# One operation over two neighbouring PSUM banks, for ScalarE's exponentials and VectorE's maxima in two attention stages

## The chip, the cores and the metric

The kernel runs on one core of a Trainium2 chip. The metric is the device time of one execution in microseconds (us). The five engines run their own queues and meet at semaphores: PE (TensorE) writes matmul results to PSUM, ACT (ScalarE) and DVE (VectorE) read PSUM and write SBUF, POOL (GpSimd) and SP (SyncE) have nothing to do in the two stages of this case.

PSUM holds eight banks here, each of 512 fp32 values per partition. A bank is filled by PE, signalled full, emptied by ACT or DVE, and signalled done.

## The reference, cut to what matters

Four layers run one after the other on x of 32 x 256 rows of 128 values (64 tiles of 128 rows): a delta-rule attention, a mixture of experts, a sliding-window attention and a full attention with a second mixture. Only the two softmax attentions are touched:

```python
# sliding window, W = 64 keys per query, 16 heads of 8
scores = jnp.einsum('blhd,blwhd->blwh', q, k_win) * dh ** (-0.5)
attn = jax.nn.softmax(scores, axis=2)
out = jnp.einsum('blwh,blwhd->blhd', attn, v_win).reshape(b, l, d)
...
# full attention inside each sequence of 256, 16 heads of 8
scores = jnp.einsum('bqhd,bkhd->bhqk', q, k) / np.sqrt(DK)
attn = jax.nn.softmax(scores, axis=-1)
o = jnp.einsum('bhqk,bkhd->bqhd', attn, v).reshape(B, S, D)
```

## The kernel before, in words

`attention_stage` is called twice, as the window stage (names ending in `_win`) and as the full stage (`_full`). Each walks 64 tiles of 128 rows; two tiles make a turn (one sequence of 256), two turns a loop body. The scores are computed twice per tile. `scores` puts queries on partitions, so that DVE can take each query's largest score (`maxima`); the maxima are turned (`turn_tops`) and added to the queries through a spare row (`tops`). `turned_scores` then computes keys on partitions with that maximum already taken off, ACT takes the exponential (`exponentials`), and `weigh` multiplies by the values. The row sums come out of a column of ones in `va`; `turn_back` and `normalize_out` divide by them.

The 16 heads lie in 4 groups (GROUPS) of 4 slots. A fill of scores takes four banks at once, one for each group. In the window stage a tile has one such fill of each kind (SF = TF = 4), in the full stage two (SF = TF = 8).

What sets the order is written out by hand: each engine has its own program, and four rings of banks with a full and a done counter each. The `scores` ring uses banks 2, 3, 0, 1, the `turned_scores` ring banks 2, 3, 4, 5; so banks 2 and 3 serve both. Bank 6 goes to ACT (`am`), bank 7 to DVE (`dv`). `scores` waits until the first two banks of the last turned fill are done (`st.filled - 2`), and `turned_scores` until the first two of the last scores fill are (`sc.filled - 2`). `fill_together` waits for all four of its own ring's last fill, `weigh` and `turn_tops` wait for all banks of a tile. Every one of these thresholds is an even number of banks.

In a tile of the full stage PE's order is: second scores (L2597), `turn_back` (L2655), either two query projections (L2556) or the turning of h (L2549), second turned scores (L2626), `turn_tops` (L2662), `turn_on` (L2668), the next first scores (L2597), `weigh` (L2646), first turned scores (L2626), `project_out` (L2674, L2676), then values (L2570) or keys and queries (L2563, L2556). The maxima are L2834 in the full stage and L2831 in the window stage, the exponentials L2765. Below, a tile that turns h is called an h tile, one that projects queries a q tile; they alternate, so that there are 32 of each.

Of the kernel before, what the change touches and what calls it, by code (L numbers as in the profile page):

```python
# [15 lines left out]
F32 = mybir.dt.float32  # L16
BF16 = mybir.dt.bfloat16
ACT = mybir.ActivationFunctionType
AX = mybir.AxisListType.X

P = 128
# [62 lines left out]
def start_signals(engine, *signals):  # L84

    for s in signals:
        engine.sem_inc(s.sem, s.per)
# [2267 lines left out]
SEQ = TPB * P  # L2355
GROUPS = 4
SLOTS = H1 // GROUPS
SETS = 2
GROUP = P // GROUPS
TOP_ROW = 2 * DH  # L2360
# [95 lines left out]
def attention_stage(nc, c, x_all, mid, w, tiles, tag, window, take=None):  # L2456
# [15 lines left out]
    KEYS = 2 * WIN - 1 if window else P  # L2472
    SCALE = DH ** -0.5
    SF, TF = (4, 4) if window else (8, 8)
    VB = 4 if window else 2
    with ExitStack() as ctx:
        def sb(name, shape, dt=F32):
            return ctx.enter_context(nc.sbuf_tensor(f"{name}_{tag}", shape, dt))
# [20 lines left out]
        mxp = sb("mxp", [P, SLOTS, P])  # L2499
        pr = sb("pr", [P, 2, TF, 512])  # L2500
# [7 lines left out]
        with ExitStack() as early:  # L2508
# [1 line left out]
                                zeros=(wq, wk, qb, va, mxp, hT, mr[:, :, tiles:], x_all[:, tiles + 1:, :],  # L2510
                                       x_all[:, 0, :], *(() if mid is None else (mean[:, :, 0], mid[:, 0, :]))),
                                ones=(oT, ones))
        bank = [ctx.enter_context(nc.psum_tensor(f"bank_{tag}_{i}", [P, 512], F32)) for i in range(8)]

        sc = Ring(ctx, nc, f"scores_{tag}", [bank[i] for i in (2, 3, 0, 1)], SF * U, ahead=SF + 4)
        st = Ring(ctx, nc, f"turned_{tag}", bank[2:6], TF * U, ahead=4)
# [220 lines left out]
        @block.scalar  # L2737
        def _(act):
            start_signals(act, st.done, am.done)

            def turned_h(b):
                bk = am.empty(act, b)
                if window:
                    nc.scalar.activation(hT[:, LEAD:], bk[:, 0:SEQ], ACT.Copy).then_inc(am.done.sem, 1)
                else:
                    nc.scalar.activation(hT[:, :], bk[:, 0:SEQ], ACT.Identity, scale=w["ln"][:, 0:1],
                                         bias=w["ln"][:, 1:2]).then_inc(am.done.sem, 1)

            def queries(b, p, half):
                bk = am.empty(act, b)  # L2750
                if window:
                    nc.scalar.activation(q[:, p, 2 * half:2 * half + 2, :],
                                         bk[:, :].rearrange("p (s n) -> p s n", s=2), ACT.Copy).then_inc(am.done.sem, 1)
                else:
                    for i in range(2):
                        slot = 2 * half + i
                        ins = nc.scalar.activation(q[:, p, slot, :], bk[:, i * SEQ:(i + 1) * SEQ], ACT.Identity,
                                                   bias=qb[:, slot:slot + 1])
                    ins.then_inc(am.done.sem, 1)

            def exponentials(b, u, n):
                for _ in range(n):
                    i = st.emptied % TF
                    bk = st.empty(act, b)
                    nc.scalar.activation(pr[0:KEYS, u % 2, i, :], bk[0:KEYS, :], ACT.Exp, scale=SCALE  # L2765
                                         ).then_inc(st.done.sem, 1)

            def copy(b, dst):
                bk = am.empty(act, b)
                nc.scalar.activation(dst, bk[:, 0:dst.shape[-1]], ACT.Copy).then_inc(am.done.sem, 1)  # L2770

            turned_h(0)
            queries(0, 0, 0)
            queries(0, 0, 1)
            turned_h(0)
            queries(0, 1, 0)
            exponentials(0, 0, 4)
            with act.Fori(0, bodies) as b:
                for u in range(U):
                    p, t = u // TPB % 2, u % TPB  # L2780
                    if t == 0:
                        queries(b, 1 - p, 1)
                    else:
                        turned_h(b)
                    if not window:
                        exponentials(b, u, 4)
                    copy(b, onT[:, :])
                    copy(b, oT[:, :])
                    exponentials(b, u + 1, 4)
                    if t == 1:  # L2790
                        queries(b, p, 0)
            copy(bodies - 1, onT[:, :])

        @block.vector
        def _(dve):
# [28 lines left out]
                    ins.then_inc(dv.done.sem, 1)  # L2824

            def maxima(b, first):
                for g in range(GROUPS):
                    bk = sc.empty(dve, b)
                    at = g * GROUP + TOP_ROW
                    if window:  # L2830
                        dve.tensor_reduce(mxp[:, :, at], bk[:, 0:SLOTS * KEYS].rearrange("p (s k) -> p s k", s=SLOTS),  # L2831
                                          AX, ALU.max).then_inc(sc.done.sem, 1)
                    else:
                        dve.tensor_reduce(mxp[:, 2 * first:2 * first + 2, at],  # L2834
                                          bk[:, :].rearrange("p (s k) -> p s k", s=2), AX, ALU.max
                                          ).then_inc(sc.done.sem, 1)

            def tops(b, u):

# [33 lines left out]
            for i in range(SF // 4):  # L2873
                maxima(0, i)
            tops(0, 0)
            keys(0, 1)
            maxima(0, 0)
            with dve.Fori(0, bodies) as b:
                for u in range(U):
                    turn, t = divmod(u, TPB)  # L2880
                    p = turn % 2
                    if not window:
                        maxima(b, 1)
                    normalize_out(b, u + 1)
                    tops(b, u + 1)
                    maxima(b, 0)
                    add_out(b, u, u)
                    if t == 0:
                        values(b, 1 - p)
                        norm_h(b, turn + 2, am_use(u - 1, "hT") if u else 4)  # L2890
                    else:
                        keys(b, p)
# [6 lines left out]
def window_stage(nc, c, x_all, a, tiles, take):  # L2899
    with ExitStack() as ctx:  # L2900
# [20 lines left out]
        with ExitStack() as s:  # L2921
# [15 lines left out]
            def _(pe):  # L2937
# [3 lines left out]
        w = {"wq": wt[:, 0, :], "wk": wt[:, 1, :], "wv": wt[:, 2, :], "wo": wo[:, :], "last_k": last_k,  # L2941
             "last_v": last_v}
        attention_stage(nc, c, x_all, None, w, tiles, "win", True, take)


def full_stage(nc, c, x_all, mid_all, a, tiles):
    with ExitStack() as ctx:
# [9 lines left out]
        with ExitStack() as s:  # L2957
# [4 lines left out]
            def _(dve):  # L2962
# [13 lines left out]
        w = {"wq": wqkv[:, 0:P], "wk": wqkv[:, P:2 * P], "wv": wqkv[:, 2 * P:], "wo": wo[:, :], "ob": ob[:, :],  # L2976
             "vb": vb[:, :], "qkb": qkb, "ln": ln}
        attention_stage(nc, c, x_all, mid_all, w, tiles, "full", False)


# [155 lines left out]
```

## Time and profile before

| what | before |
|---|---|
| median of 3 runs | 7614.07 us |
| all three | 7606.62, 7614.07, 7653.81 us |
| profiled execution | 7602.55 us, its span 7600.8 us |
| busy in the span | PE 84%, DVE 51%, ACT 41% |
| maxima, full stage | 524 of 685 ns |
| exponentials, full stage | 516 of 602 ns |
| maxima, window stage | 264 of 681 ns |
| exponentials, window stage | 260 of 602 ns |

A time is the whole execution; the span is the profiled part of it, and 1.75 us lie around it. Of the span, the window stage's tiles take from about 5420 to 6150 us and the full stage's from about 6205 to 6994 us; the rest belongs to the other stages.

### The profile page before, as it was taken

The numbers are of one execution on the slowest core, as the hardware profiler recorded it, in microseconds if no ns is written. First come the engines' busy times: TensorE is split into PE (matmuls) and PEld (weight loads), VectorE is DVE, ScalarE is ACT, GpSimd is POOL, SyncE is SP. The second block draws the span as 40 slices with busy tenths as digits, with TensorE's granted clock in tenths as the row PEclk, the third lists the DMA queues.
The fourth block names the chain that finished last, engine by engine and source line by source line (L and its number), as shares of the span: only waits on it lengthen the run. The fifth ranks groups of instructions, "written<-read, shape, count | busy, mean of one in ns | idle before, by whom it ended". The sixth has DMA issues, their size and how long they took to land. (4 is left out here: it accounts for less than half of the span.)

```text
span 7600.8 us, 186089 instructions
## 1 busy us (share of the span) xinstructions
PE 6383.9 (84%) x68255; PEld 4549.0 (60%) x68256; DVE 3882.0 (51%) x7259; ACT 3145.8 (41%) x6176; POOL 1951.7 (26%) x1826
## 2 busy tenths in 40 slices
PE   2889999998999999999999999967588868887577
PEld 2566666666666666666666666646366646665477
DVE  3445545555455554555555555455444446666433
ACT  0444444444444444444444444414233325554155
POOL 2323223232232322223223232234100010001554
PEclk8999999999999999999999999979799989998588
DMA  3910000000000000000000000011100000000114
GB/s 101 322 35 1 2 1 1 1 1 2 1 1 2 1 2 1 1 1 1 2 1 1 2 1 1 1 35 50 33 0 0 0 2 0 0 0 22 36 56 117
DMA packets 92899, 160.08 MB, mean 21 GB/s; under 512 B 14156, under 2 KB 75636, under 8 KB 89588
## 3 DMA queue, kind: packets, MB, share of 16 engines
q1 hardware_dynamic: 70036, 121.89, 5.4%
q0 software_dynamic: 14080, 26.64, 1.0%
q8 instruction: 435, 7.13, 0.4%
q10 hardware_dynamic: 8320, 4.19, 0.2%
q14 instruction: 28, 0.23, 0.0%
HBM read 119.30 MB, written 104.06 MB: 29 GB/s over the span
## 5 line engine op out<-in xcount | busy, mean ns | idle before, releaser
L677 PE MATMUL bank<-wc,hT 128*128 128x512 f32 x3144 | 1517.6, 607 | 89.3 <-issue 83.9
L677 PEld LDWEIGHTS bank<-wc,hT 128*128 128x128 f32 x3144 | 557.8, 190 | 576.5 <-issue 560.8
L816 PE MATMUL bank<-X,kqe 128*128 128x64 f32 x6240 | 774.2, 277 | 74.9 <-DVE rb L1253 54.3
L816 PEld LDWEIGHTS bank<-X,kqe 128*128 128x128 f32 x6240 | 726.3, 192 | 98.9 <-DVE rb L1253 69.9
L1230 DVE TENSOR_TENSOR kqe<-bank,ex 128x512 f32<-128x512 f32 x520 | 335.1, 686 | 760.6 <-PE bank L723 760.6
L1285 DVE TENSOR_TENSOR yb<-bank,masks 128x512 bf16<-128x512 f32 x768 | 525.9, 685 | 234.9 <-PE bank L779 234.9
L1018 ACT ACTIVATE TT<-bank 128x512 bf16<-128x512 f32 x640 | 382.3, 597 | 539.0 <-PE bank L797 536.6
L1018 ACT ACTIVATE ex<-bank 128x512 bf16<-128x512 f32 x640 | 346.8, 594 | 392.4 <-PE bank L790 392.4
L949 ACT ACTIVATE th<-bank 128x512 f32<-128x512 f32 x523 | 304.7, 597 | 425.5 <-PE bank L677 409.0
L779 PEld LDWEIGHTS bank<-ex,mTb 128*128 128x128 bf16 x6144 | 253.7, 99 | 321.6 <-ACT ex L1018 185.7
L1125 POOL TENSOR_SCALAR_AFFINE_SELECT kqe<-kqe 128x512 f32<-128x512 f32 x260 | 215.7, 830 | 786.5 <-DVE kqe L1230 786.5
L779 PE MATMUL bank<-ex,mTb 128*128 128x64 bf16 x6144 | 309.7, 193 | 108.1 <-ACT ex L1018 78.4
L2834 DVE TENSOR_REDUCE mxp_full<-bank_full 128x2 f32<-128x512 f32 x524 | 325.7, 685 | 88.8 <-PE bank_full L2597 87.0
L1094 POOL TENSOR_TENSOR rs<-rs,halves 128x32 f32<-128x32 f32 x65 | 354.9, 5460 | 11.9 <-POOL rs L1093 11.9
L1093 POOL TENSOR_SCALAR rs<-ss 128x32 f32<-128x32 f32 x65 | 19.5, 300 | 1314.1 <-DVE ss L1189 1314.1
L1106 POOL TENSOR_TENSOR z<-z,o_rows 128x1024 f32<-128x1024 f32 x66 | 209.6, 3176 | 521.2 <-DVE z L1184 521.0
L980 ACT ACTIVATE ex<-bank 128x512 f32<-128x512 f32 x260 | 157.2, 604 | 436.4 <-DVE kqe L1230 398.6
L1253 DVE TENSOR_TENSOR rb<-v,bank 128x512 bf16<-128x512 f32 x260 | 179.1, 689 | 274.7 <-PE bank L816 274.7
L2765 ACT ACTIVATE pr_full<-bank_full 128x512 f32<-128x512 f32 x516 | 266.4, 602 | 75.0 <-PE bank_full L2626 75.0
L723 PE MATMUL bank<-kqT,kbT 64*128 64x256 f32 x2080 | 294.9, 402 | 0.0
L1277 DVE TENSOR_TENSOR ex<-bank,mask 128x512 bf16<-128x512 f32 x256 | 165.0, 686 | 245.3 <-PE bank L759 245.3
L723 PEld LDWEIGHTS bank<-kqT,kbT 64*128 64x128 f32 x2080 | 178.9, 186 | 170.3 <-issue 158.7
(511 smaller groups left out, 12883.3 us busy)
## 6 DMA issues: line engine op xcount, KB each, us to landing
sent_l0f<-blank_l0f SPq DMA_DIRECT2D x8, 4224.0 KB, 62.9
sent_l1m<-blank_l1m SPq DMA_DIRECT2D x8, 4224.0 KB, 134.7
xin<-sent_l1m SPq DMA_DIRECT2D x139, 66.0 KB
taken_l1m<-back_l1m SPq DMA_DIRECT2D x16, 512.0 KB, 8.7
cw_stage<-in_L_attn_conv_w_dram SPq DMA_DIRECT2D x6, 1024.0 KB, 5.5
xin<-sent_l0f SPq DMA_DIRECT2D x75, 66.0 KB
out_dram<-x_sb ACTq DMA_DIRECT2D x8, 512.0 KB, 7.4
back_l1m<-y,xin POOLq DMA_INDIRECT x136
```

The costliest lines, as they stand in the source:

```text
L677: mm = pe.matmul(bk[:, :], src[:, j:j + P], w["wc"][:, j, at * 512:(at + 1) * 512], start=(j == 0), stop=(j == TAPS - 1))
L723: mm = pe.matmul(bk[:, i * 256:(i + 1) * 256], kbT[rows(hh), hh // 2, :], kqT[rows(hh), hh // 2, :, :].rearrange("p a n -> p (a n)"), star ...
L779: mm = pe.matmul(bk[:, i * HALF:(i + 1) * HALF], mTb[:, hh, :], left(T[:, hh, :], l), start=True, stop=True)
L816: mm = pe.matmul(bk[:, i * D0:(i + 1) * D0], lhsT(hh), rhs(hh), start=True, stop=True)
L949: nc.scalar.activation(th[:, n % 2, :], proj.banks[n % 2][:, :], ACT.Tanh, scale=1.0 if ch[0] == "v" else 0.5).then_inc(th_ready.sem, 1)
L1018: nc.scalar.activation(dst, bk[:, :].rearrange("p (h a u) -> p h a u", h=8, u=1 << l), ACT.Copy).then_inc(actb.done.sem, 1)
L1094: pool.tensor_tensor(rs[:, f % TPB, :, :], rs[:, f % TPB, :, :], c["halves"][:, 0:2 * H0].rearrange("p (a h) -> p a h", a=2), ALU.pow).the ...
L1125: pool.affine_select(out=v, in_=v, compare_op=ALU.not_equal, fill=1.0, base=0, pattern=[[0, HB], [-1, P]], channel_multiplier=1).then_inc( ...
L1230: dve.tensor_tensor(kqe[1 - t % 2][:, i // 2 * HB + i % 2:i // 2 * HB + HB:2, :, :], bk[:, :].rearrange("p (h a n) -> p h a n", h=2, a=2), ...
L1285: dve.tensor_tensor(group(yb, G), bk[:, :].rearrange("p (a n) -> p a n", n=HALF), c["masks"][:, l, :].unsqueeze(1).to_broadcast([P, 8, HAL ...
L2765: nc.scalar.activation(pr[0:KEYS, u % 2, i, :], bk[0:KEYS, :], ACT.Exp, scale=SCALE).then_inc(st.done.sem, 1)
L2834: dve.tensor_reduce(mxp[:, 2 * first:2 * first + 2, at], bk[:, :].rearrange("p (s k) -> p s k", s=2), AX, ALU.max).then_inc(sc.done.sem, 1)
```

## The change

The eight banks are now declared as four tensors of two banks each, and `bank[i]` is a view of half of one. The rings, their order of banks, all thresholds and all matmuls stay. `exponentials` counts off two banks of its ring (two waits) and then issues one ACTIVATE over both, which raises the done counter by two. `maxima` does the same with one TENSOR_REDUCE.

```diff
-        bank = [ctx.enter_context(nc.psum_tensor(f"bank_{tag}_{i}", [P, 512], F32)) for i in range(8)]
+        pair = [ctx.enter_context(nc.psum_tensor(f"banks_{tag}_{i}", [P, 2, 512], F32)) for i in range(4)]
+        bank = [pair[i // 2][:, i % 2, :] for i in range(8)]
...
             def exponentials(b, u, n):
-                for _ in range(n):
+                for _ in range(n // 2):
                     i = st.emptied % TF
-                    bk = st.empty(act, b)
-                    nc.scalar.activation(pr[0:KEYS, u % 2, i, :], bk[0:KEYS, :], ACT.Exp, scale=SCALE
-                                         ).then_inc(st.done.sem, 1)
+                    st.empty(act, b)
+                    st.empty(act, b)
+                    nc.scalar.activation(pr[0:KEYS, u % 2, i:i + 2, :], pair[1 + i // 2 % 2][0:KEYS, :, :], ACT.Exp,
+                                         scale=SCALE).then_inc(st.done.sem, 2)
...
             def maxima(b, first):
-                for g in range(GROUPS):
-                    bk = sc.empty(dve, b)
-                    at = g * GROUP + TOP_ROW
-                    if window:
-                        dve.tensor_reduce(mxp[:, :, at], bk[:, 0:SLOTS * KEYS].rearrange("p (s k) -> p s k", s=SLOTS),
-                                          AX, ALU.max).then_inc(sc.done.sem, 1)
-                    else:
-                        dve.tensor_reduce(mxp[:, 2 * first:2 * first + 2, at],
-                                          bk[:, :].rearrange("p (s k) -> p s k", s=2), AX, ALU.max
-                                          ).then_inc(sc.done.sem, 1)
+                for g in range(0, GROUPS, 2):
+                    sc.empty(dve, b)
+                    sc.empty(dve, b)
+                    two, at = pair[1 - g // 2], slice(g * GROUP + TOP_ROW, (g + 2) * GROUP, GROUP)
+                    to = mxp[:, :, at] if window else mxp[:, 2 * first:2 * first + 2, at]
+                    n = SLOTS if window else 2
+                    dve.tensor_reduce(to.rearrange("p s g -> p g s"), two[:, :, 0:n * (KEYS if window else SEQ)].rearrange(
+                        "p g (s k) -> p g s k", s=n), AX, ALU.max).then_inc(sc.done.sem, 2)
```

On ACT, in the loop of the full stage, between the exponentials and the next work for `weigh` (`pr` holds the exponentials, `onT` the turned output of the tile before, `oT` the weighed values). Before:

```order
L2765 ACTIVATE pr_full<-bank_full 128x512
L76 REGISTER_ALU
L2765 ACTIVATE pr_full<-bank_full 128x512
L76 REGISTER_ALU
L2765 ACTIVATE pr_full<-bank_full 128x512
L76 REGISTER_ALU
L2765 ACTIVATE pr_full<-bank_full 128x512
L76 REGISTER_ALU
L2770 ACTIVATE onT_full<-bank_full 128x128
```

The same place with the change:

```order
L76 REGISTER_ALU x2
L2768 ACTIVATE pr_full<-banks_full 128x1024
L76 REGISTER_ALU x2
L2768 ACTIVATE pr_full<-banks_full 128x1024
L76 REGISTER_ALU
L2773 ACTIVATE onT_full<-banks_full 128x128
```

Four ACTIVATEs of 512 have become two of 1024. Each of the new ones has two register operations ahead of it, one for each bank's count, and the first count is waited for between the two.

On DVE, in the loop of the full stage, the maxima of the second scores and the work behind them (`rc` and `on` are the reciprocals and the normalized output). The change's rows:

```order
L76 REGISTER_ALU x2
L2836 TENSOR_REDUCE mxp_full<-banks_full 128x2x2
L76 REGISTER_ALU x2
L2836 TENSOR_REDUCE mxp_full<-banks_full 128x2x2
L76 REGISTER_ALU
L2850 RECIPROCAL rc_full<-banks_full 128x16
```

Where two TENSOR_REDUCEs stand there were four, each with one register operation ahead; what follows keeps its place. Each new one writes two maxima for each of two banks. PE's order is the same on both sides.

## Rows read from the trace of the kernel before

**Rows 1.** Busy time by stage: engines' us (instructions), granted clock, DMA share, GB/s.

```profile
core 0: us, PE busy (x) PEld busy (x) DVE busy (x) ACT busy (x) POOL busy (x), PEclk, DMA share, GB/s
5420.00:6150.00 730.00, 618.15 (x12348) 439.46 (x12346) 325.02 (x684) 241.38 (x485) 0.00 (x0) 0.98 0.00 0
6205.00:6994.00 789.00, 693.59 (x9698) 507.92 (x9698) 509.64 (x1076) 390.87 (x812) 0.00 (x0) 0.95 0.00 0
```

**Rows 2.** Waits, full stage, 6300 to 6900 us: total us, times, longest us.

```profile
PE bank_full L2662 <- DVE on_full L2851: 25.8, 50, 0.5
...
PE bank_full L2626 <- DVE mxp_full L2834: 13.9, 25, 0.6
...
PEld bank_full L2597 <- ACT pr_full L2765: 6.7, 37, 0.3
```

**Rows 3.** Waits, window stage, 5500 to 6100 us, the same columns.

```profile
PE bank_win L2610 <- DVE mxp_win L2831: 16.2, 55, 0.3
```

**Rows 4.** Timeline, an h tile of the full stage: start, duration, operation, idle before.

```profile
6646.34 1.15 PE L2597 MATMUL bank_full<-kT_full,q_full 17*128 17x256 f32 x16
...
6647.51 2.49 DVE L2834 TENSOR_REDUCE mxp_full<-bank_full 128x2 f32<-128x512 f32 x4
...
6647.91 0.38 PE L2549 MATMUL bank_full<-ident,h_full 128*128 128x128 f32 x2
6648.33 0.56 ACT L2746 ACTIVATE hT_full<-bank_full,ln 128x256 f32<-128x256 f32 x1 [1.72 <-PE bank_full L2549]
...
6648.85 1.15 PE L2626 MATMUL bank_full<-q_full,kT_full 17*128 17x256 f32 x16 [0.56 <-DVE mxp_full L2834]
...
6650.01 2.06 ACT L2765 ACTIVATE pr_full<-bank_full 128x512 f32<-128x512 f32 x4 [1.12 <-PE bank_full L2626]
...
6650.53 0.66 PE L2662 MATMUL bank_full<-ident,mxp_full 128*128 128x128 f32 x4 [0.54 <-DVE on_full L2851]
...
6651.03 0.27 PE L2668 MATMUL bank_full<-ident,on_full 128*128 128x128 f32 x1
...
6651.23 1.15 PE L2597 MATMUL bank_full<-kT_full,q_full 17*128 17x256 f32 x16
...
6652.31 1.96 PE L2646 MATMUL bank_full<-pr_full,va_full 128*32 128x128 f32 x64
```

**Rows 5.** Timeline, the q tile behind it.

```profile
6661.01 1.15 PE L2626 MATMUL bank_full<-q_full,kT_full 17*128 17x256 f32 x16
...
6662.17 2.06 ACT L2765 ACTIVATE pr_full<-bank_full 128x512 f32<-128x512 f32 x4 [0.27 <-PE bank_full L2626]
...
6663.31 0.74 PEld L2597 LDWEIGHTS bank_full<-kT_full,q_full 17*128 17x128 f32 x16 [0.17 <-ACT pr_full L2765]
```

**Rows 6.** Timeline, a tile of the window stage.

```profile
5709.73 2.47 DVE L2831 TENSOR_REDUCE mxp_win<-bank_win 128x4 f32<-128x508 f32 x4 [1.96 <-PE bank_win L2588]
...
5711.06 1.08 PE L2610 MATMUL bank_win<-bandT_win,identb 128*127 128x512 bf16 x4 [0.29 <-DVE mxp_win L2831]
```

**Rows 7.** Groups of instructions, DVE: count, busy us, mean ns, idle before.

```profile
L1189 DVE TENSOR_REDUCE ss<-kbT 128x16 f32<-128x1024 f32 x130 | 158.1, 1216 | 35.9 <-ACT kbT L960 34.8 <-ACT kbT L956 1.1
```

**Rows 8.** Groups of instructions, ACT, the same columns.

```profile
L2765 ACT ACTIVATE pr_full<-bank_full 128x512 f32<-128x512 f32 x516 | 266.4, 602 | 75.0 <-PE bank_full L2626 75.0
...
L1010 ACT ACTIVATE rb<-v 128x1024 bf16<-128x1024 f32 x65 | 67.6, 1041 | 0.0
...
L376 ACT ACTIVATE gate_tmp<-gate_tmp 128x1024 f32<-128x1024 f32 x1 | 1.1, 1056 | 2.3 <-DVE gate_tmp L415 2.3
```

**Rows 9.** Timeline, gate computation: an ACTIVATE with two waits ahead of it.

```profile
98.79 1.12 PE L334 MATMUL gate_tb<-ident,gate_h 128*128 128x128 f32 x4 [1.65 <-DVE gate_h L394]
100.02 0.60 ACT L363 ACTIVATE gate_hT<-gate_tb 128x512 f32<-128x512 f32 x1 [3.72 <-PE gate_tb L334]
```

**Rows 10.** Page, section 5: the maxima, columns as in rows 7.

```profile
L2834 DVE TENSOR_REDUCE mxp_full<-bank_full 128x2 f32<-128x512 f32 x524 | 325.7, 685 | 88.8 <-PE bank_full L2597 87.0
```

**Rows 11.** Busy time around one fall of the clock in the window stage, columns as in rows 1.

```profile
5516.00:5521.00 5.00, 4.57 (x63) 3.13 (x68) 1.78 (x6) 0.66 (x2) 0.00 (x0) 0.66 0.00 0
```

## The prediction

> **What bounds the kernel now.** I read the busy time by stage first, then the waits, then the timeline of single tiles. Only two stages are touched: the window stage with 730 us and the full stage with 789 us [rows 1], together a fifth of the span. In both, PE is by far the busiest (618 of 730 us, 694 of 789), DVE second and ACT third. So a shorter operation on DVE or ACT is worth nothing by itself; it is worth something only where PE stands still for it. The waits name the places. In the full stage PE waits for the maxima ahead of L2626 (13.9 us in 25 times, so in every h tile of that stretch and in no q tile), for `on_full` ahead of L2662 (25.8 us in 50, every tile), and its weight load waits for the exponentials ahead of L2597 (6.7 us in 37) [rows 2]. In the window stage PE waits for the maxima ahead of L2610, 16.2 us in 55 times, 0.29 us a tile [rows 3].
>
> The timeline of an h tile shows how these hang together [rows 4]. The scores end at 6647.49 (6646.34 and 1.15), four maxima run from 6647.51 for 2.49 us, and PE starts the turned scores at 6648.85: that is when two of the four are done. Their exponentials start at 6650.01, and the next scores at 6651.23, again when two of four are done. Beside this runs a second path: all four maxima end at 6650.00, the output is normalized behind them, then L2662 at 6650.53, L2668 at 6651.03, and L2597 0.20 us later. Both paths reach L2597 within about a tenth of a microsecond. In a q tile PE is busy with queries while the maxima run, L2626 starts with no wait shown, and only the exponentials (6662.17) hold L2597 (6663.31) [rows 5]. `weigh` (L2646) starts 1.08 us after the scores [rows 4], nearly their whole length; I take it to be bound by PE.
>
> **The change part by part.**
> What is awaited is nearly always the first pair of a block of four, since the thresholds are `filled - 2`. So two numbers matter for each engine: when the first pair is given back, and when all four are.
>
> *Maxima now.* One takes 0.685 us [rows 10], four take 2.49 [rows 4], so the starts lie (2.49 - 0.685) / 3 = 0.602 apart and each overlaps the next by 0.083. First pair: 0.602 + 0.685 = 1.287 us after the start. All four: 2.49.
>
> *Maxima after.* The nearest row is a TENSOR_REDUCE over 1024 elements, 1.216 us [rows 7]; it reads SBUF, not two banks, and I take 1.22. With the same overlap two of them last 1.22 - 0.083 + 1.22 = 2.36.
>
> *Exponentials now.* 0.602 each [rows 8], four in 2.06 [rows 4]: starts 0.486 apart, overlap 0.116. First pair 1.088, all four 2.06.
>
> *Exponentials after.* Rows of 1024 elements take 1.041 and 1.056 [rows 8]; I take 1.05. Two last 1.05 - 0.116 + 1.05 = 1.98.
>
> *The later start.* The first operation no longer starts when its first bank is full. It waits for the count of bank one, then executes a register operation, then waits for bank two. No row shows this pair of waits at this place. Lower bound 0: the wait for bank two is met at once and the register operation costs nothing. Upper bound from two rows: an ACTIVATE behind one wait starts 0.04 us after PE's end (6648.29 to 6648.33) [rows 4], one behind two waits 0.11 after it (99.91 to 100.02) [rows 9], 0.07 more; and bank two may be full later than bank one by a fill's matmul pitch, at most 1.15 / 16 = 0.07 [rows 4], of which part passes beside the register operation; I cap the sum at 0.11. I take 0.04, since sixteen matmuls in 1.15 us must run side by side and end nearly together, so that only the register operation is left.
>
> *First pair, net.* DVE: 1.287 - (0.04 + 1.22) = 0.03 us earlier (bounds 0.07 earlier, 0.04 later). ACT: 1.088 - (0.04 + 1.05) = 0.00 (bounds 0.04 earlier, 0.07 later). All four: DVE 2.49 - 2.40 = 0.09 earlier, ACT 2.06 - 2.02 = 0.04.
>
> The row for ACT differs from a rule here. The Trainium skill, ScalarE: Activation LUTs, section What ACT_TABLE_LOAD costs, gives an ACTIVATE with immediate scale and bias as 186 ns + 0.833 ns per element and lets neighbours overlap by about 93 ns. By that the first pair is given back at 0.520 + 0.613 = 1.133 now and at 0.04 + 1.039 = 1.079 after, 0.054 earlier, and 64 tiles would add an estimated 3.5 us to the gain. The trace does not agree with its overlap: it shows 0.602 a piece and 0.116.
>
> *Window stage.* PE's wait of 0.29 us a tile ends with the first pair of maxima [rows 6]: 64 x 0.03 = 1.9 us. The exponentials there have several matmul blocks of time before anyone needs them; nothing.
>
> *Full stage.* In an h tile the two first pairs stand in a chain: 0.03 + 0.00 = 0.03, and the second path to L2597 gains 0.09, so it does not take over. In a q tile 0.00. Sum 32 x 0.03 = 1.0 us. The wait ahead of L2662 gets shorter by 0.09 but what follows it is then held by the exponentials: next late is ACT's first pair, in both kinds of tile.
>
> *Given back together.* A bank is now given back with its neighbour. No wait of PE asks for an odd number of banks, so none is lengthened by it; had one done so, it would cost half a pair. The register operations stay as many as before; half of the ACTIVATEs and TENSOR_REDUCEs go. The stage prologues have 3 blocks of maxima and one of exponentials; below 0.5 us. No DMA, PE instruction, POOL or SP instruction moves.
>
> Sum: 1.9 + 1.0 = 2.9 us less. Against the profiled execution's 7602.55 that is 7599.6. The median of the runs shown, 7614.07, lies 11.5 above it with 7653.81 as the third run; the three executions that agree (7602.55, 7606.62, 7614.07) have a mean of 7607.7, which I take as the base: 7607.7 - 2.9 = 7605.
>
> **The rivals.**
> 1. *Every saved microsecond counts.* If DVE and ACT were the bound, each pair of maxima would bring 2 x 0.602 - 1.137 = 0.067 us and each pair of exponentials 2 x 0.486 - 0.934 = 0.038, over 394 and 388 pairs 26 + 15 = 41 us: 7567. A milder form has no later start at all: 64 x 0.07 in the window stage, 32 x (0.07 + 0.04) + 32 x 0.04 in the full stage, 9 us: 7598. For it: the waits of rows 2 name both engines. Against the strong form: PE's busy share in both stages. Chance 0.14, nearly all of it for the mild form.
> 2. *Slower: two banks cost as two operations.* If a read that crosses from one bank to the next saves nothing, a pair costs 2 x 0.685 = 1.37 and 2 x 0.602 = 1.20, it can't overlap inside, and with the start 0.11 later the first pair comes 0.19 and 0.23 us later. Exposed are 96 first pairs of maxima (64 window tiles, 32 h tiles) and 64 of exponentials: 18 + 15 = 33 us more, 7641. Against it: 1024 elements from SBUF cost 1.22 and 1.05 [rows 7, 8]; for it: no row reads two banks. It decides from a pair of 1.29 us on DVE or 1.09 on ACT; for 1% of the time, 76 us, each exposed pair would have to come 0.48 us later. Chance 0.12 in all, with milder forms (only the start is late, 0.11: 96 x 0.04 + 64 x 0.07, 8 us, 7616) holding most.
> 3. *The clock moves.* The granted clock is 0.98 in the window stage and 0.95 in the full stage [rows 1], in short falls to the lower level, 1.2 GHz, such as five microseconds at 0.66 [rows 11], worth up to 0.34 x 5 = 1.7 us. PE waited a little oftener ahead of them in every tile, and the tile's pattern changes by hundredths of a microsecond. All falls together are worth at most 0.02 x 730 + 0.05 x 789 = 54 us; half of them gone or half more is 27 us either way: 7578 or 7632. Chance 0.14, both sides alike.
> 4. *The change doesn't do what it says*: the order shows both merged forms, so this keeps 0.01.
>
> **How the numbers follow.** Forecast 0.59, the rivals 0.14, 0.12, 0.14 and 0.01. The likeliest gives 7605. The range reaches to the clock's two ends, 7578 and 7632, which takes in the bounds of the unknown start (7598 to 7616) and the scatter of executions (7602.55 to 7614.07); left out are the strong forms of rivals 1 and 2. About 1% (76 us) is what a measurement of this kernel tells from no change. No case reaches it worked out from rows: faster needs more than all pairs together, slower needs 0.48 us for each exposed pair. I keep 0.03 for each.
>
> **What would show it.** The merged operations at 1.22 and 1.05 us, blocks of two at about 2.36 and 1.98; longer ones point to rival 2. In the h tile, L2626 about 1.31 us behind the start of DVE's old block instead of 1.34; the wait ahead of L2662 shorter by about 0.09; the wait ahead of L2597 for the exponentials longer or in more tiles. Window wait L2610 down from 0.29 to about 0.26. If the maxima start more than 0.05 us later behind the end of the scores than now, the later start was mis-sized. The prediction is wrong if the stages' lengths differ by more than some microseconds with an unchanged clock.

## The result and the profile after

| | before | after |
|---|---|---|
| median of 13 runs | 7605.10 us | 7652.01 us |
| lowest and highest | 7595.15, 7653.81 | 7638.55, 7679.44 |
| ratio | 1 | 1.0064, interval 1.0049 to 1.0080 |
| profiled execution, its span | 7602.55, 7600.8 us | 7665.74, 7664.0 us |
| first to last output projection, window stage | 699.2 us | 698.3 us |
| the same, full stage | 747.8 us | 797.0 us |

The change makes the kernel about 47 us slower, 0.6%. That is under the 1% named in the prediction, but clear of the measurement's own uncertainty and outside the range of 7578 to 7632. In the profiled executions the full stage is 49.2 us longer, the window stage 0.9 shorter; another 14 lie ahead of the window stage, where nothing was changed and where executions differ by as much. The medians' difference is about that of the full stage. (The stretch ahead of the window stage isn't the change's: of two later kernels with the change in them, fill_h and fill_q, it is some 3 us shorter than before.)

The page of the kernel after, its head and the first section (before: 186089 instructions too, DVE x7259, ACT x6176):

```profile
span 7664.0 us, 186089 instructions
## 1 busy us (share of the span) xinstructions
PE 6429.4 (84%) x68255; PEld 4580.7 (60%) x68256; DVE 3855.9 (50%) x6865; ACT 3119.6 (41%) x5788; POOL 1948.5 (25%) x1826
```

DVE has 394 operations fewer and ACT 388, and the whole program as many instructions as before. So 782 others were added. They are not busy time, but the view of line L76, the helper that waits for a bank, counts them; before, it has no EVENT_SEMAPHORE:

```profile
L76 DVEq EVENT_SEMAPHORE  x394: 21/21/50, 5435.7 to 7050.7; - x197
L76 ACTq EVENT_SEMAPHORE  x388: 17/17/38, 5451.6 to 7053.6; - x194
```

One stands ahead of each merged operation. What it is for, the experiments show.

The merged operations, groups of ACT and DVE [rows 8, 10]:

```profile
L2768 ACT ACTIVATE pr_full<-banks_full 128x1024 f32<-128x1024 f32 x258 | 250.0, 1021 | 100.3 <-PE banks_full L2628 100.3
...
L2836 DVE TENSOR_REDUCE mxp_full<-banks_full 128x4 f32<-128x1024 f32 x262 | 308.9, 1221 | 131.0 <-PE banks_full L2599 131.0
```

1.221 and 1.021 us: the durations came as priced, ACT's a little shorter. Now the same h tile as in [rows 4], the timeline of the kernel after:

```profile
6664.33 1.15 PE L2599 MATMUL banks_full<-kT_full,q_full 17*128 17x256 f32 x16
...
6665.65 2.36 DVE L2836 TENSOR_REDUCE mxp_full<-banks_full 128x4 f32<-128x1024 f32 x2 [0.22 <-PE banks_full L2599]
...
6666.94 1.15 PE L2628 MATMUL banks_full<-q_full,kT_full 17*128 17x256 f32 x16 [0.65 <-DVE mxp_full L2836]
...
6668.23 1.94 ACT L2768 ACTIVATE pr_full<-banks_full 128x1024 f32<-128x1024 f32 x2 [1.35 <-PE banks_full L2628]
...
6668.56 0.66 PE L2664 MATMUL banks_full<-ident,mxp_full 128*128 128x128 f32 x4 [0.47 <-DVE on_full L2852]
...
6669.31 1.61 PE L2599 MATMUL banks_full<-kT_full,q_full 17*128 17x256 f32 x16
6670.85 3.10 PE L2648 MATMUL banks_full<-pr_full,va_full 128*32 128x128 f32 x64
```

The scores end at 6665.48 and the maxima start at 6665.65, 0.17 us later; before it was 0.02. The exponentials start 0.14 behind PE's end (6668.09); before 0.01. The blocks are shorter, 2.36 and 1.94 us in place of 2.49 and 2.06, but the first pair is what is waited for: from the start of the scores to that of the turned scores it now takes 2.61 us, before 2.51. PE waits 0.65 us for the maxima and then 0.47 for the output, before 0.56 and 0.54. And in the last two rows the same matmuls take 1.61 and 3.10 us in place of 1.15 and 1.96. The clock has fallen.

How often, the busy time of five stretches of 51 us shows (PE, PEld, DVE, ACT, POOL, granted clock, DMA):

```profile
6640.00:6691.00 51.00, 45.45 (x601) 33.16 (x600) 29.99 (x51) 23.05 (x34) 0.00 (x0) 0.90 0.00 0
6691.00:6742.00 51.00, 44.31 (x621) 32.26 (x620) 32.48 (x54) 24.48 (x36) 0.00 (x0) 0.96 0.00 0
6742.00:6793.00 51.00, 45.41 (x601) 32.96 (x600) 30.14 (x50) 22.89 (x35) 0.00 (x0) 0.90 0.00 0
6793.00:6844.00 51.00, 45.44 (x602) 32.99 (x601) 30.15 (x50) 22.89 (x35) 0.00 (x0) 0.90 0.00 0
6844.00:6895.00 51.00, 45.44 (x601) 32.98 (x600) 30.14 (x50) 22.90 (x35) 0.00 (x0) 0.90 0.00 0
```

A loop body of four tiles with its falls takes 51 us, and four of these five lose the same tenth; the second has one fall fewer. The starts of one DVE line (L2865) give the tiles' lengths:

```profile
6688.22 0.29 DVE L2865 TENSOR_TENSOR mid<-mid,banks_full 128x128 f32 x1 [1.03 <-PE banks_full L2678]
6699.12 0.29 DVE L2865 TENSOR_TENSOR mid<-mid,banks_full 128x128 f32 x1 [1.01 <-PE banks_full L2678]
6711.38 0.29 DVE L2865 TENSOR_TENSOR mid<-mid,banks_full 128x128 f32 x1 [1.00 <-PE banks_full L2678]
6723.89 0.29 DVE L2865 TENSOR_TENSOR mid<-mid,banks_full 128x128 f32 x1 [1.93 <-PE banks_full L2678]
6736.26 0.29 DVE L2865 TENSOR_TENSOR mid<-mid,banks_full 128x128 f32 x1 [1.02 <-PE banks_full L2678]
6750.26 0.29 DVE L2865 TENSOR_TENSOR mid<-mid,banks_full 128x128 f32 x1 [2.69 <-PE banks_full L2678]
```

An h tile takes 10.90 us at the upper level, 12.51 with a short fall in it, and 14.00 with a long one; q tiles take 12.26 to 12.37 (before 12.15 to 12.23 at the upper level). At the upper level an h tile took 10.80 before. So 0.1 us of a tile is the change's, and 1.6 to 3.1 us in nearly every h tile the clock's: in the whole stage the clock falls 29 times in 32 h tiles, and before 11 times.

### The profile page after: what moved, and what is told of

It reads as the page before. It is cut to its first block and busy times, and to the rows that moved or that the text cites. A ratio compares the mean times of both kernels' runs of the same rounds, so it can differ in the third digit from the quotient of the medians.

```text
span 7664.0 us, 186089 instructions
## 1 busy us (share of the span) xinstructions
PE 6429.4 (84%) x68255; PEld 4580.7 (60%) x68256; DVE 3855.9 (50%) x6865; ACT 3119.6 (41%) x5788; POOL 1948.5 (25%) x1826
## 5 line engine op out<-in xcount | busy, mean ns | idle before, releaser
L2836 DVE TENSOR_REDUCE mxp_full<-banks_full 128x4 f32<-128x1024 f32 x262 | 308.9, 1221 | 131.0 <-PE banks_full L2599 131.0
L2768 ACT ACTIVATE pr_full<-banks_full 128x1024 f32<-128x1024 f32 x258 | 250.0, 1021 | 100.3 <-PE banks_full L2628 100.3
```

The source lines that it names most:

```text
L2768: nc.scalar.activation(pr[0:KEYS, u % 2, i:i + 2, :], pair[1 + i // 2 % 2][0:KEYS, :, :], ACT.Exp, scale=SCALE).then_inc(st.done.sem, 2)
L2836: dve.tensor_reduce(to.rearrange("p s g -> p g s"), two[:, :, 0:n * (KEYS if window else SEQ)].rearrange("p g (s k) -> p g s k", s=n), AX, ...
```

## The experiments

Each kernel was compared with the kernel before on its own chip; between these chips the kernel before differs (7606, 7579, 7563 and 7611 us), so ratios and differences are what can be compared. "Full" is the full stage from first to last output projection, in the profiled execution, with the mean granted clock of 6300 to 6900 us. "Window" is the same of the window stage. Both columns rest on one traced execution of each kernel. The diffs are cut to the lines that matter; what stands behind a # in them is a note for the reader.

| kernel | time, before beside it | ratio (interval) | window | full, clock |
|---|---|---|---|---|
| before | | 1 | 699.2 | 747.8, 0.96 |
| after | 7652.0, 7605.1 | 1.0064 (1.0049 to 1.0080) | 698.3 | 797.0, 0.91 |
| one_wait | 7605.1, 7606.5 | 1.0001 (0.9991 to 1.0012) | 699.0 | 743.5, 0.97 |
| exp_only | 7607.7, 7606.5 | 0.9999 (0.9989 to 1.0010) | 699.1 | 742.6, 0.97 |
| max_only | 7625.1, 7606.5 | 1.0027 (1.0017 to 1.0038) | 699.5 | 766.7, 0.94 |
| waits_only | 7642.4, 7606.5 | 1.0052 (1.0038 to 1.0065) | 698.3 | 774.5, 0.94 |
| inc_one | 7563.0, 7578.7 | 0.9985 (0.9976 to 0.9995) | 692.0 | 751.7, 0.96 |
| fill_after | 7553.1, 7578.7 | 0.9966 (0.9955 to 0.9978) | 699.4 | 729.8, 1.00 |
| fill_before | 7550.7, 7578.7 | 0.9960 (0.9948 to 0.9972) | 698.1 | 723.2, 1.00 |
| fill_h | 7557.2, 7578.7 | 0.9976 (0.9967 to 0.9985) | 698.5 | 729.5, 1.00 |
| fill_q | 7610.6, 7562.9 | 1.0054 (1.0036 to 1.0072) | 699.1 | 789.6, 0.93 |
| best_before | 7527.5, 7562.9 | 0.9944 (0.9930 to 0.9958) | 679.6 | 722.9, 1.00 |
| best_inc | 7519.1, 7562.9 | 0.9940 (0.9925 to 0.9956) | 670.3 | 722.5, 1.00 |
| rise_two | 7663.3, 7610.5 | 1.0066 (1.0049 to 1.0084) | 698.8 | 797.2, 0.91 |

### Is it the start or the merging?

**one_wait.** The change with one wait for a pair:

```diff
-                    st.empty(act, b)
-                    st.empty(act, b)
+                    st.empty_two(act, b)      # one wait, for full.at(turn, n + 2); maxima alike
```

> The change with one wait for each pair (for the second bank's count) in place of two. Theory A (the two waits in a row start each block late, and the granted clock multiplies that): the maxima start at most 0.10 us behind the modelled end of the scores (0.02 before, 0.17 with the change), an h tile's L2626 starts no later behind the start of its scores than before (2.51 us), clean tiles are at most as long as before (10.56 and 11.4 us in the window stage, 10.80 and 12.2 in the full stage), the full stage's mean clock is 0.95 or more, the time within 10 us of the kernel before. Theory B (merging itself costs: two banks given back together, or read by one operation): tiles stay at 10.66 and 11.5 us, full stage clock 0.89, time 45 to 60 us above before, as with the change.

The loss is gone, as theory A had it, but not each number: the maxima start 0.13 us behind the scores' end (expected 0.10 at most), and an h tile's turned scores 2.57 us behind the scores' start (expected no more than the 2.51 of before). Timeline of one_wait:

```profile
6657.11 1.15 PE L2605 MATMUL banks_full<-kT_full,q_full 17*128 17x256 f32 x16
...
6658.39 2.36 DVE L2840 TENSOR_REDUCE mxp_full<-banks_full 128x4 f32<-128x1024 f32 x2 [0.17 <-PE banks_full L2605]
...
6659.68 1.15 PE L2634 MATMUL banks_full<-q_full,kT_full 17*128 17x256 f32 x16 [0.61 <-DVE mxp_full L2840]
```

Removing one of the two waits took away 0.04 us of the start, and with it all of the 47 us, as far as the runs tell. So the loss is not in proportion to the delay, and 0.11 us of late start were still unexplained.

**exp_only** and **max_only** each take one half of the change (`maxima`, or `exponentials`, from the kernel before).

> Only the exponentials in pairs, the maxima as before. Theory A: window tiles stay at 10.56 and 11.4 us, since PE waits for no exponential there; in the full stage only the exponentials' first pair is late, by 0.06 us a tile, half to two thirds of the change's lengthening; the clock falls oftener than before, 15 to 50 us in all. If the clock's falls in the full stage hang on the maxima's wait alone, 0 to 10 us.

> Only the maxima in pairs, the exponentials as before. Theory A: window tiles 0.10 us longer as with the change, with few or no falls of the clock there; in the full stage h tiles about 0.08 us longer, q tiles unchanged; full stage clock between 0.89 and 0.95; 10 to 50 us above before. Theory B: the same, so this run and exp_only only share the cost out between the two engines.

The exponentials alone cost nothing, though they too start late (nor, then, does declaring the banks in pairs, which exp_only does too); the 15 to 50 us expected of theory A were wrong, and the other case named there (0 to 10 us, if the falls hang on the maxima's wait) came true. The maxima alone cost 0.27%, 19 us, within the 10 to 50 expected, and in the trace the full stage is 766.7 us. The exponentials' part costs nothing, the maxima's 19 us, both together 47: not a sum.

**waits_only** keeps operations of 512 and waits for both banks ahead of each pair.

```diff
+                    two = [st.empty(act, b), st.empty(act, b)]
+                    for k in range(2):
+                        nc.scalar.activation(pr[0:KEYS, u % 2, i + k, :], two[k][0:KEYS, :], ACT.Exp, scale=SCALE
+                                             ).then_inc(st.done.sem, 1)
```

> The change's waits without its merging: operations of 512 as before, but ahead of each pair both banks are waited for, in two waits. Theory A: the start is 0.15 us late and nothing is saved behind it, so the first pair of maxima comes 0.15 us later than before and that of exponentials 0.13; window tiles 0.15 us longer than before (10.7 and 11.55), the full stage at least as long as with the change (797 us from first to last output projection), time 45 us or more above before. Theory B: as the kernel before, within 10 us.

36 us slower with nothing merged: theory B falls. Theory A's sizes were missed too: 45 us or more and a full stage of at least 797 were expected. Its maxima start 0.10 us behind the scores, 0.09 later than before where 0.15 was expected:

```profile
6650.56 1.15 PE L2597 MATMUL bank_full<-kT_full,q_full 17*128 17x256 f32 x16
6651.81 2.49 DVE L2836 TENSOR_REDUCE mxp_full<-bank_full 128x2 f32<-128x512 f32 x4
```

The same two waits with a wide operation behind them gave 0.17. So something that comes with the wide operation starts late beside the two waits. And the full stage (774.5) is shorter than the change's although two of its tiles at the upper level take 23.3 us, with the change 23.15: more proof that the falls, not the delay, make the sum.

### What else starts late

**inc_one.** The traces' operand texts showed a difference: an operation that raises a counter by one carries its wait itself; where it raises it by two, the wait is an instruction of its own ahead of it. This kernel has one wait per pair and done counters that count pairs:

```diff
+class Halved(Signal):                     # per // 2, and at(turn, n) gives super().at(turn, n // 2)
...
+        sc.done, st.done = Halved(...), Halved(...)
-                                         scale=SCALE).then_inc(st.done.sem, 2)
+                                         scale=SCALE).then_inc(st.done.sem, 1)
```

> The change with one wait for each pair, and with done counters that count pairs, so that the merged operation raises its counter by one. In the traces so far an operation that raises a counter by one carries its own wait, one that raises it by two has the wait as an instruction of its own ahead of it; against the last matmul's start the first maxima start at 0.392 us before, 0.480 with the two waits alone, 0.510 with one wait and a rise by two, 0.555 with the change. Theory A2 (the late start is made of register operation, separate wait and bank two): the maxima start at 0.43 to 0.45, the exponentials at 0.43 (before 0.391, change 0.524), clean tiles at or up to 0.05 us below those of the kernel before (10.56 and 11.37 in the window stage, 10.80 and 12.2 in the full stage), the time from 10 us below the kernel before to 3 above it. Rival (the wide operation itself starts late, because of its longer pattern): starts stay at 0.51 and 0.49, tiles as with one_wait, time as before.

The page's head:

```profile
span 7559.2 us, 184587 instructions
```

and the timeline:

```profile
6608.52 1.15 PE L2616 MATMUL banks_full<-kT_full,q_full 17*128 17x256 f32 x16
6609.73 2.36 DVE L2851 TENSOR_REDUCE mxp_full<-banks_full 128x4 f32<-128x1024 f32 x2
...
6612.21 1.94 ACT L2784 ACTIVATE pr_full<-banks_full 128x1024 f32<-128x1024 f32 x2 [1.14 <-PE banks_full L2645]
```

The maxima start 0.06 us behind the scores' end, the exponentials 0.05. Against the last matmul's start it is 0.434 and 0.433 us, inside what was expected. The kernel is 0.15% faster than before, 15.7 us, where at most 10 was expected. That the gain is the merging's isn't shown: in the traces it lies wholly in the window stage (692.0 for 699.2 us); in the full stage a q tile and an h tile at the upper level take 22.97 us together, before 22.98. The halved counters also changed PE's own instructions, 48 fewer in the trace. What is shown is that with a rise by one and one wait the kernel with merged operations is no slower.

**rise_two** puts it the other way round: the kernel before, nothing merged, counters raised by two and thresholds doubled.

```diff
+class Doubled(Signal):                    # per * 2, and at(turn, n) gives super().at(turn, n * 2)
...
-                                         ).then_inc(st.done.sem, 1)
+                                         ).then_inc(st.done.sem, 2)     # maxima alike
```

> The kernel before, nothing merged, every maximum and exponential of the two stages raising its done counter by two and all thresholds on it doubled. Theory A2 (a rise by two puts the wait into an instruction of its own): the page's count of instructions grows by 1564 (784 maxima and 780 exponentials, less the 24 or so in the prologues that never carried a wait), with the same count of matmuls, ACTIVATEs and TENSOR_REDUCEs; the maxima start 0.06 to 0.07 us later behind the end of the scores than the 0.02 us before, the exponentials 0.06 later; tiles get 0.05 to 0.10 us longer in the window stage per tile and 0.06 to 0.12 in the full stage, 7 to 12 us in all at an unchanged clock. Rival: the late start of the wide operations comes from their width; then nothing moves here, instructions and times as before.

Page and timeline of rise_two:

```profile
span 7667.7 us, 187733 instructions
...
PE 6439.9 (84%) x68255; PEld 4587.5 (60%) x68256; DVE 3882.8 (51%) x7259; ACT 3143.6 (41%) x6176; POOL 1946.7 (25%) x1826
```

```profile
6661.56 1.15 PE L2607 MATMUL bank_full<-kT_full,q_full 17*128 17x256 f32 x16
6662.79 2.49 DVE L2844 TENSOR_REDUCE mxp_full<-bank_full 128x2 f32<-128x512 f32 x4
6664.14 1.15 PE L2636 MATMUL bank_full<-q_full,kT_full 17*128 17x256 f32 x16 [0.64 <-DVE mxp_full L2844]
```

The same operations, 1644 instructions more, maxima 0.08 us behind the scores instead of 0.02, and 0.66% slower: as much as the whole change. The view of the helper's line, now L85, shows what came:

```profile
L85 DVEq EVENT_SEMAPHORE  x788: 21/21/21, 5436.5 to 7049.6; - x197
L85 ACTq EVENT_SEMAPHORE  x776: 17/17/17, 5452.4 to 7054.2; - x194
```

That is one for every maximum and every exponential, and exactly the 1564 expected; the other 80 are in PE's sequencer, whose thresholds were doubled, so that PE's program isn't quite the same. The size was missed, for I expected 7 to 12 us at an unchanged clock, and the clock did not stay: 0.91 in the full stage, with 29 falls. The window tiles hardly lengthened (two take 21.99 us on average at the upper level, before 21.96); PE's wait for the maxima there grew from 0.29 to 0.36 us, and its waits for DVE elsewhere shrank by about as much.

The starts behind the modelled end of the matmuls, DVE and ACT: before 0.02 and 0.01; rise_two 0.08 and 0.07; waits_only 0.10 and 0.09; inc_one 0.06 and 0.05; one_wait 0.13 and 0.11; after 0.17 and 0.14. Counted from the last matmul's start, which is recorded and not modelled, the maxima start at 0.392 us before and at 0.555 after, 0.16 later; the exponentials 0.13. So waiting for bank two costs 0.04, the wait as its own instruction 0.06 to 0.08, and the second of the two waits 0.03 to 0.05 more.

The loss doesn't go by the start alone. From the start of an h tile's scores to that of its turned scores, and so with the first pair's duration in it, it takes 2.51 us before and in exp_only, 2.49 in inc_one and 2.57 in one_wait: these spend 38 to 61 us of the full stage at the lower level, by the clock's record. It takes 2.58 in rise_two, 2.60 in waits_only and 2.61 in max_only and after: these spend 143, 89, 82 and 143 us there. So one_wait's maxima start later than rise_two's, but its first pair is shorter and PE waits a little less, 0.61 us for 0.64; that this small difference decides between the two is what the numbers suggest, not what a run shows. Within the second group the time at the lower level does not follow the wait.

### Is it the clock?

**fill_after**, **fill_before** and **fill_h** put matmuls that compute nothing where PE waits in the full stage; their banks are PE's at that time and are overwritten after.

```diff
+                banks = st.fill_together(pe, b, GROUPS)
+                if t and chunk and not window:
+                    pe.matmul(banks[2][:, 0:SEQ], c["ident"][:, :], wq[:, 0:2, :], start=True, stop=True)
                 pe.wait_ge(sc.done.sem, sc.done.at(b, sc.filled - 2))
-                banks = st.fill_together(pe, b, GROUPS)
...
                 pe.wait_ge(sc.done.sem, sc.done.at(b, SF * (u + 1)))
+                if not window:                                        # not in fill_h
+                    pe.matmul(sc.banks[2][:, 0:P], c["ident"][:, :], wq[:, 0, :], start=True, stop=True)
                 bk = dv.fill(pe, b)
```

> The change, with matmuls that compute nothing put where PE waits in the full stage: one of 256 columns ahead of the turned scores of an h tile (wait of 0.66 us), one of 128 columns ahead of the turning of the maxima in every tile (wait of 0.47 us). Theory C (most of the loss is the granted clock, which falls behind these waits): the clock falls in the full stage rarely or not at all (before 11 times, with the change 29 times between the first and last output projection), its mean there goes from 0.91 to 0.99 or more, the full stage takes about 745 us in place of 802, and the time falls to 7590 to 7605 although work was added. Rival C2 (the clock's falls have nothing to do with these waits): falls stay, each tile is longer by what the matmuls don't hide, 0 to 0.2 us, time 7650 to 7670.

> The kernel before with the same empty matmuls in PE's waits of the full stage. Theory C: its 11 falls there (51 us at the lower level) go too, 10 to 20 us faster than the kernel before. If fill_after and fill_before then differ by 4 to 10 us, that is what the late start costs by itself at an unchanged clock. Rival C2: as the kernel before or up to 13 us slower.

> The change with the first of the two matmuls only, in the wait of the h tile ahead of the turned scores. Theory C with the place of the fall right behind the h tile's two waits: most of the 29 falls go, time 7600 to 7625. If the shorter wait ahead of the turning of the maxima is what matters: 7640 or more.

Busy time of all three, 6300 to 6900 us; first fill_after:

```profile
6300.00:6900.00 600.00, 564.37 (x7936) 409.36 (x7935) 389.47 (x647) 298.30 (x440) 0.00 (x0) 1.00 0.00 0
```

then fill_before and fill_h:

```profile
6300.00:6900.00 600.00, 566.09 (x7984) 412.63 (x7983) 407.21 (x864) 314.48 (x654) 0.00 (x0) 1.00 0.00 0
...
6300.00:6900.00 600.00, 540.32 (x7844) 394.03 (x7844) 390.59 (x647) 298.54 (x441) 0.00 (x0) 1.00 0.00 0
```

Not one fall is left, in any of the three, and TensorE does more and is done sooner. The wait of the h tile alone is enough, and it need not be filled whole: in fill_h 0.22 us of the 0.65 are left. The gains were larger than expected: fill_before is 28 us below the kernel before (expected 10 to 20), fill_h 21.5 us (expected little or nothing). That fill_h is a little above fill_after in time lies within what the runs scatter. This splits the full stage's 49.2 us. At an unchanged clock the change costs 729.8 - 723.2 = 6.6 us. The clock takes 797.0 - 729.8 = 67.2 us with the change and 747.8 - 723.2 = 24.6 without it: 42.6 us more. The split rests on single traces, but two things bear it out: the empty matmuls leave the tiles at the upper level as long as they were (two take 22.97 us in fill_before and 22.98 before), and the clock's record has 143.4 us at the lower level after and 51.2 before, half of which, lost at half the clock, is 71.7 and 25.6. The medians of fill_after and fill_before differ by 2.4 us, with overlapping intervals.

**fill_q** puts the same matmul where PE does not wait, in the q tiles (`t == 0`).

> The change with the empty matmul of 256 columns in the q tiles, where PE is not waiting, and none in the h tiles' waits. It adds TensorE work and lengthens a q tile by 0.2 to 0.5 us, 6 to 16 us in all. Theory C (the clock falls because PE stands in the h tile's waits): the falls in the full stage stay near the change's 29, time 5 to 20 us above the change (so 50 to 70 above the kernel before). Theory D (what counts is how the loop body's length, 51.15 us with its two falls, meets the clock's own rhythm): the body is now 0.4 to 1.0 us longer, the falls drop to the 11 to 19 of the other kernels, and the time is below the change's despite the added work.

It adds work on the path, 0.3 to 0.35 us in a q tile, and the full stage is 7.4 us shorter than the change's, with 19 falls for 29 in the clock's record. In time it is not told apart from the change (1.0054 and 1.0064, overlapping intervals). So neither theory came out whole: C expected as many falls as with the change and a longer time, D a time below the change's. The falls that stay fit C: the same matmul away from the waits doesn't take them away. And since fill_q moves the wait for its own banks ahead of the other just as the other fills do, it is the filled wait that counts in those, and not the moved one. That there are 19 and not 29 falls fits D, that their number hangs also on the length of the loop body; but it is one trace. With the waits in place, at 51 us a body, they come in nearly every body. Why just there I haven't shown.

### A faster version

**best_before** and **best_inc** add fill_h's matmul, and in the window stage issue the mask matmuls of banks 4 and 5 ahead of the wait for banks 2 and 3, to the kernel before and to inc_one.

```diff
-                pe.wait_ge(sc.done.sem, sc.done.at(b, sc.filled - 2))
...
-                    for bk in banks:
+                    for g in (2, 3, 0, 1):
+                        bk = banks[g]
+                        if g == 0:
+                            pe.wait_ge(sc.done.sem, sc.done.at(b, sc.filled - 2))
```

> The kernel before with two additions: the empty matmul of 256 columns in the h tile's wait, and in the window stage the mask matmuls of banks 4 and 5 issued ahead of the wait for banks 2 and 3. Theory: PE's wait of 0.29 us a tile in the window stage (L2610) is covered by 0.5 us of matmuls it has to do anyway, so a window tile gets 0.25 to 0.29 us shorter, 16 to 18 us in all; the full stage has no falls, 24 us less. Time 35 to 45 us below the kernel before. Rival: the maxima's next use takes over as the wait in the window stage, only 0.1 us a tile.

> inc_one (pairs, one wait, counters raised by one) with the same two additions. If what merging saves is still on the path: 3 to 8 us below best_before (full stage 0.07 us per two tiles shorter, window tiles no longer tied to the maxima). If nothing of it is left on the path once PE's waits are filled: equal to best_before within 3 us.

Both beat either kernel: 35 and 44 us below the kernel before. A tile of best_inc's window stage:

```profile
5708.88 2.34 DVE L2857 TENSOR_REDUCE mxp_win<-banks_win 128x8 f32<-128x1016 f32 x2 [1.40 <-PE banks_win L2607]
5709.81 1.08 PE L2635 MATMUL banks_win<-bandT_win,identb 128*127 128x512 bf16 x4
```

The wait ahead of the mask matmuls is gone [rows 6]; the window stage is 19.6 us shorter in best_before (16 to 18 expected) and 28.9 in best_inc. Between the two versions lie 9 us in the window stage's trace and nothing in the full stage's, and as with inc_one it isn't shown that they are the merging's; in time their intervals overlap (0.9930 to 0.9958 and 0.9925 to 0.9956), so which is faster stays open.

## Why the prediction was wrong

- **What is waited for** held: only the first pair of a block counts, the blocks' shorter length brings nothing by itself, and the places were those named.
- **The durations** held: 1.22 and 1.02 against 1.22 and 1.05.
- **The failing step is the later start.** The text took 0.04 us, "so that only the register operation is left", and capped it at 0.11. It is 0.16 on DVE and 0.13 on ACT. Bank two (0.04) and the second wait (0.03 to 0.05) were in the list; the largest part was not: raising the counter by two drives the wait out of the operation. The order lists ahead of the prediction show register operations but no waits, so this difference isn't in them; the program's count of instructions shows it, the same on both sides though 782 operations went. With 0.16 and 0.13 the text's own sum gives a first pair of maxima 0.16 + 1.22 - 1.287 = 0.09 us later and of exponentials 0.13 + 1.02 - 1.088 = 0.06 later, where it had 0.03 earlier and 0.00: 64 x 0.09 + 32 x 0.15 + 32 x 0.06 = 12.5 us more in place of 2.9 less. So this term alone turned the sign. Measured at an unchanged clock: 6.6 us in the full stage, and in the window stage 22.17 us for two tiles in place of 21.96, 6.7 us. That the window stage is no longer for it is luck: before, the clock fell six times there, after not once.
- **The clock rival** was the right mechanism with too small a price. The text let half of the falls come or go, 27 us, and gave it no link to the main term. The runs show that they hang together: 42.6 us of the full stage's 49.2 are falls that come with the delay of about 0.1 us a tile, and go when the wait is filled. It is this term that takes the time out of the range: at an unchanged clock both stages together cost 13 us, from 7605 to 7618. Rival 3 named the tile's changed pattern, but took both signs as equally likely.
- **Rival 2** (two banks cost as two operations) did not happen; its milder form, a late start, had the right sign, and 8 us where 13 were measured at an unchanged clock.
- **The Trainium skill**, ScalarE: Activation LUTs, section What ACT_TABLE_LOAD costs, gives, worked out from its figures, an estimate of 1.039 us for a merged exponential; the trace gives 1.021, close to it.

## What to carry to other kernels

Merging two operations shortens the block and can delay its first result, since both inputs are waited for; where the first result is what the next engine waits for, work out that one time, with every instruction between the last signal and the start. Count the instructions of the whole program on both sides: here a semaphore rise of two cost an extra instruction for each operation that waits. And where TensorE's waits sit close to what makes its clock fall, a tenth of a microsecond a tile can cost several times its own sum (here 42.6 us beside 6.6), and an empty matmul in the wait can give more than the optimization.

## What the runs showed of the hardware

- An operation that waits on one semaphore and raises another by one carries both in these programs. A rise by two alone, with nothing merged, put 1564 waits into instructions of their own on DVE and ACT (1644 more in all) and added 0.66% of the time (rise_two).
- The granted clock stayed at its upper level through a stage whose PE waits of 0.66 us in every second tile were filled in part with a 256-column matmul; unfilled it fell 8 to 29 times in the nine kernels traced, though no wait of PE in that stage was longer than 0.66 us before and after.
- One operation over two banks takes less than two operations over one each: 1.221 us for 1024 elements on DVE against 0.685 for 512, 1.021 against 0.602 on ACT.
- Not settled: in inc_one a window h tile is 0.08 us shorter at a place ahead of `turn_back`, where PE waits behind the copy of the values, which the change doesn't touch; rise_two too gained there. No run was made for it.
